# Attention and routed experts on one core: maxima placed in halves of a batch, second scores six steps behind the first

## The chip, the cores and the metric

The kernel runs on one core of one Trainium2 chip. The metric is the device time of one execution in microseconds. Engines: PE multiplies matrices, DVE (vector), ACT (scalar) and POOL (GpSimd) work on tiles, SP starts transfers. Each engine runs its own list of instructions in order and meets the others only through semaphores.

## The reference, cut to what matters

```python
# x, ctx: (8, 256, 256); 16 heads of 16; 8 experts, top 2, hidden width 1024
x = x + attention(layernorm(x), ctx, ctx)          # scores, softmax over keys, values, Wo, bo
h = layernorm(x)
gate = softmax(h @ w_gate.T)                       # choose 2 of 8 experts for each of 2048 tokens
y = sum over chosen e of gate_e * (gelu(h @ W1[e] + b1[e]) @ W2[e] + b2[e])
out = x + y
```

## The kernel before, in words

**Attention** goes over 8 batches of 256 tokens. The 16 heads of a batch are taken in 8 pairs, and a pair is one *step*, so that steps 0 to 63 hold the first scores of all pairs. In step s PE computes the scores of pair s into `S1` (`scores_for_max`, L1318), and DVE takes each query's maximum (`take_max`, L863) and stores it in `nmax`. PE cannot start the next `S1` before DVE has read this one. When a batch's 8 pairs are through, `maxima` (L872, L874) splits the 8 columns of maxima in two parts into `mrep`, PE turns them (`turn_maxima`, L1294), ACT copies them to `mT`, and a DMA from ACT's queue puts them into spare rows of the stacked queries `Q` (`maxima_out`, L1124). With these rows in place, a second product gives scores that already have the maximum taken off.

That product (`scores`, L1341, into `S2`) runs `LAG = 10` steps behind: step s holds the second scores of pair s - 10. ACT takes the exponential into `prob` (L1143), PE multiplies by the values two steps later, for two pairs at once (`weighted`, L1353), and ACT takes the sums out (`sums_out`, tile `OT`).

**Everything else is placed by tables of step numbers.** `FRONT` places a batch's loads, norm and projections (`xn` L1270, `q` and `k` L1278, `v` L1286) relative to step 8n. `BACK` and `LATE_BACK` place what follows the sums: division (`div` L1361, `divide`), turn and output projection (`ao`, `o`), residual (`add`), second norm (`ln2`, `norm2`), turn (`y`). `ROUTE` and `LATE_ROUTE` place the routing of groups of batches, (0, 1), (2, 3), (4), (5), (6), (7): `logits` L1370, `choose`, `gates`, `tags`, `count` L1385, `places` L947, `rows` L965, and `scatter` (L575), in which POOL issues one indirect DMA for each of 2 halves and 2 choices of a batch, so 4 for a batch, 8 for a group of two. Each engine's program walks the same steps and writes, in a fixed order within the step, what the table names. Nothing but semaphores ties engines to a step: an engine whose next work is ready goes on.

Batch 7 has its first scores in steps 56 to 63 and its second in 66 to 73. In steps 0 to 9, where there are no second scores, PE also runs matmuls that nobody reads (`unread`, L1391): 12 in step 0, 3 in each of the others.

**Experts** start at `UNIT_STEP = 76`: 23 tiles of up to 256 rows, each in 4 units (`pe_unit`, L1218 and L1233), one unit a step until step 99 and the rest after it. The expert and first row of a tile come from a table that DVE works out when the groups before it are routed (`LISTED`: the first 5 tiles after group 3 at step 70, two more after group 4, the others after group 5). SP loads rows and weights of a tile at the steps of `SP_TILES` (tiles 0 and 1 at step 71).

## Time and profile before

| | us |
|---|---|
| median of 3 runs (lowest, highest) | 524.69 (522.09, 527.28) |
| profiled execution | 525.33 |
| its span, first to last instruction | 524.0 |
| PE / DVE / ACT / POOL busy in the span | 457.9 / 360.4 / 334.8 / 165.2 |
| first `S1` matmul, last `S1` matmul | 23.7, 185.4 |
| last exponential, first expert matmul | 233.3, 241.7 |

The span is what the profiler saw of one execution. A busy share of PE is not PE at its peak, since matmuls overlap in its pipeline and their ends are modelled.

### The profile page before, as it was taken

How to read it: one execution, taken by the hardware profiler on the slowest of the kernel's cores; microseconds unless marked ns; L12 is line 12 of the kernel's file. 1: busy time of each engine (PE TensorE's matmuls, PEld its weight loads, DVE VectorE, ACT ScalarE, POOL GpSimd, SP SyncE). 2: the span in 40 equal slices, each digit the busy share in tenths (PEclk: the TensorE clock that was granted, in tenths of full speed). 3: DMA queues.
4: the chain of work that ended last, by engine and by line, in shares of the span. 5: the costliest groups of instructions: out<-in, count | busy, mean ns of one | idle time of the engine just before them, and what ended most of it. 6: DMA issues, size and time to landing. Idle time of an engine off the chain costs nothing.

```text
span 524.0 us, 10489 instructions
## 1 busy us (share of the span) xinstructions
PE 457.9 (87%) x3741; PEld 390.5 (75%) x3741; DVE 360.4 (69%) x791; ACT 334.8 (64%) x569; POOL 165.2 (32%) x213
## 2 busy tenths in 40 slices
PE   4897989999999844658889987999999999999993
PEld 3365666766765622427889977899999999999992
DVE  3276776776777751336977997298868788888862
ACT  1123776667666522335968856498779889889880
POOL 6023330352321577210361513132333213312323
PEclk9999999999999966665989989899999999999998
DMA  6557615324310023149275859859787987878822
GB/s 226 175 159 218 210 62 171 124 69 150 124 66 24 31 95 106 42 164 357 83 246 176 278 154 269 254 206 270 218 242 240 277 250 232 276 266 245 282 32 30
DMA packets 44356, 93.03 MB, mean 178 GB/s; under 512 B 6928, under 2 KB 30096, under 8 KB 38416
## 3 DMA queue, kind: packets, MB, share of 16 engines
q1 hardware_dynamic: 35072, 81.41, 46.3%
q0 software_dynamic: 7152, 9.46, 9.3%
q10 hardware_dynamic: 2080, 1.49, 0.9%
q8 instruction: 31, 0.51, 0.4%
q14 instruction: 21, 0.17, 0.1%
HBM read 63.01 MB, written 14.26 MB: 147 GB/s over the span
## 4 chain that ended last, share of the span: by engine, by line
PE 52%; issue 10%; DVE 10%; ACT 9%; DMA 6%; POOL 4%; another core or an unknown queue 4%; SPq 3%; ACTq 1%; DVEq 0%; POOLq 0%
PE S L1218 13%; PE bank L1233 12%; PE bank L1278 6%; PE bank L1286 5%; PE S L1318 4%; DMA w_in<-in_W 4%; PE bank L1353 3%; DVE nmax L863 3%; ACT hf L1068 2%; PE S L1391 2%; PE bank L1270 2%; PE S L1341 2%; ACT W2p L1049 2%; ACT Q L1037 1%
## 5 line engine op out<-in xcount | busy, mean ns | idle before, releaser
L1218 PE MATMUL S<-xgT,Q 128*128 128x256 f32 (+1 forms) x736 | 139.1, 289 | 8.7 <-DVE xgT L757 5.2
L534 POOL DMA_INDIRECT out<-y,slot x39 | 69.4, 1780 | 177.3 <-DVE y L781 103.7
L1218 PEld LDWEIGHTS S<-xgT,Q 128*128 128x128 f32 x736 | 117.5, 198 | 9.3 <-issue 9.3
L863 DVE TENSOR_REDUCE nmax<-S 128x4 f32<-128x1024 f32 x64 | 78.4, 1225 | 47.6 <-PE S L1318 45.1
L1218 PE MATMUL S<-xgT,K 128*128 128x256 f32 (+1 forms) x368 | 105.6, 287 | 0.0
L1068 ACT ACTIVATE hf<-S,b1c 128x256 f32<-128x256 f32 (+1 forms) x184 | 70.6, 435 | 40.2 <-PE S L1218 36.4
L1143 ACT ACTIVATE prob<-S 128x1024 f32<-128x1024 f32 x64 | 65.8, 1028 | 38.8 <-PE S L1341 27.7
L767 DVE TENSOR_TENSOR hp<-hf,hp 128x512 fp32r<-128x512 f32 (+1 forms) x92 | 55.8, 607 | 29.7 <-ACT hp L1081 29.3
L1218 PEld LDWEIGHTS S<-xgT,K 128*128 128x128 f32 x368 | 72.6, 197 | 0.0
L734 DVE TENSOR_TENSOR K<-w_in,Q 128x1024 fp32r<-128x1024 f32 x46 | 56.4, 1225 | 19.9 <-ACT Q L1037 19.9
L1233 PE MATMUL bank<-W2p,hp 128*128 128x256 f32 x528 | 67.6, 284 | 0.3 <-DVE y L777 0.3
L1233 PEld LDWEIGHTS bank<-W2p,hp 128*128 128x128 f32 x528 | 64.7, 191 | 0.6 <-issue 0.4
L554 POOL TENSOR_TENSOR rstd<-ve,half 128x2 f32<-128x2 f32 x16 | 11.8, 736 | 137.7 <-DVE ve L848 137.3
L1081 ACT ACTIVATE hp<-hf 128x512 fp32r<-128x512 f32 (+1 forms) x92 | 52.3, 569 | 2.9
L1037 ACT ACTIVATE Q<-w_in 128x1024 fp32r<-128x1024 f32 x46 | 48.2, 1048 | 8.6 <-DMA w_in<-in_W 7.5
L1233 PE MATMUL bank<-Q,hp 128*128 128x256 f32 x272 | 51.3, 282 | 1.3 <-DVE y L777 1.2
L1233 PEld LDWEIGHTS bank<-Q,hp 128*128 128x128 f32 x272 | 42.9, 188 | 1.6 <-issue 1.6
L575 POOL DMA_INDIRECT lists<-x2n,rows x32 | 31.7, 990 | 39.3 <-DVE rows L965 31.1
L1353 PE MATMUL bank<-prob,V 128*32 128x256 f32 x512 | 37.7, 416 | 1.2 <-ACT prob L1143 1.2
L1233 PE MATMUL bank<-K,hp 128*128 128x256 f32 x136 | 38.3, 282 | 0.0
L1318 PEld LDWEIGHTS S<-K,Q 64*128 64x128 f32 x256 | 19.1, 184 | 24.8 <-issue 13.2
L1318 PE MATMUL S<-K,Q 64*128 64x256 f32 x256 | 32.2, 330 | 5.7 <-DVE nmax L863 5.1
(179 smaller groups left out, 702.1 us busy)
## 6 DMA issues: line engine op xcount, KB each, us to landing
w_in<-in_W SPq DMA_DIRECT2D x46, 1024.0 KB, 7.9
K<-flat_k SPq DMA_DIRECT2D x24, 256.0 KB, 2.4
Q<-flat_q SPq DMA_DIRECT2D x24, 256.0 KB
xg<-lists SPq DMA_DIRECT2D x16, 265.0 KB
b_in<-in_b SPq DMA_DIRECT2D x23, 128.0 KB
lists<-zero SPq DMA_DIRECT2D x9, 265.0 KB, 4.9
cin<-in_ctxT SPq DMA_DIRECT2D x8, 256.0 KB, 3.5
xin<-in_x SPq DMA_DIRECT2D x8, 256.0 KB, 3.9
```

What stands on the lines that cost most here:

```text
L534: st_y[i % 4].after(pool.indirect_dma_start(out=out, out_offset=bass.IndirectOffsetOnAxis(ap=slot[i % 4][:, t:t + 1], axis=0), in_=y[i % 2 ...
L734: w1_lo.after(dve.tensor_tensor(W1p[i % 2][1][:, c], w1_in[i % 2][:, c], W1p[i % 2][0][:, c].bitcast(F32), ALU.subtract))
L767: h_lo.after(dve.tensor_tensor(hp[i % 2][1][:, c, 0:n], hf[pair % 2][:, :, 0:n], hp[i % 2][0][:, c, 0:n].bitcast(F32), ALU.subtract))
L863: max_done.after(dve.tensor_reduce(nmax[n % 4][:, :, :, m].rearrange("p t r -> p r t"), S1[:].rearrange("p r (t k) -> p r t k", t=TT), AX. ...
L1037: w1_hi.after(act.activation(W1p[i % 2][0][:, c], w1_in[i % 2][:, c], ACT.Copy))
L1068: h_act.after(act.activation(hf[pair % 2][:, u, 0:n], h_bank[pair][:, u, 0:n], ACT.Gelu, bias=b1c[i % 3][:, 2 * pair + u:2 * pair + u + 1]))
L1081: h_hi.after(act.activation(hp[i % 2][0][:, 2 * pair:2 * pair + 2, 0:n], hf[pair % 2][:, :, 0:n], ACT.Copy))
L1143: exp_done.after(act.activation(prob[s % 4][:].rearrange("p r t l -> p (r t l)"), S2[:].rearrange("p r l -> p (r l)"), ACT.Exp, scale=SCALE))
L1218: ins = pe.matmul(h_bank[pair][:, u, 0:n], W1p[k][a][:, kc, m * P:(m + 1) * P], xgT[k][c][:, kc, 0:n], start=(j == 0), stop=(j == len(term ...
L1233: ins = pe.matmul(y_bank[:, t, :], hp[k][a][:, m, t * P:(t + 1) * P], W2p[k][c][:, m, :], start=(j == 0), stop=(j == len(terms) - 1))
L1318: i = pe.matmul(S1[:, r, t * L:(t + 1) * L], Q[n % HELD][a, m, t * P:(t + 1) * P], K[n % HELD][a, m, :], start=not masked, stop=(not maske ...
L1353: i = pe.matmul(b[j * OS:(j + 1) * OS, 0:L], V[n % 3][:, t, r * MP + m, :], prob[(MP * n + m) % 4][:, r, t, :], start=(t == 0), stop=(t == ...
```

## The change: what it does

Maxima are handled in halves of a batch, 4 pairs each: `mrep0` and `mx0` after pair 3, `mrep1` and `mx1` after pair 7, each with its own turn, copy and DMA into half of the spare rows. The second scores wait for their half alone, and `LAG` is 6. The back work of a batch moves three to eight steps forward, the routing of groups 1 to 5 three to six, `UNIT_STEP`, `LAST`, `SP_TILES` and `POOL_TILES` four. Group 0 is routed 16 steps earlier, and its 8 scatters are written one to a step. Those of groups 1, 2 and 4 are written two to a step. Batches 5 and 7 are normalised on DVE, as batch 6 was. `xn` and `xT` come one step earlier, and ACT takes the values out ahead of the exponential.

```diff
-    UNIT_STEP = 76
+    UNIT_STEP = 72
-    LAG = 10
+    LAG = 6
+    MH = MP // 2
-    FRONT = dict(... xn=-8, xT=-7, ... v=-1, v_out=0, mrep=7, mx=8)
+    FRONT = dict(... xn=-9, xT=-8, ... v=-1, v_out=0)
-    BACK = dict(div=20, divide=21, ao=22, aT=23, o=27, add=28, store=30, ln2=32, norm2=33, y=34, yT=35)
+    BACK = dict(div=16, divide=17, ao=18, aT=19, o=19, add=20, store=22, ln2=24, norm2=25, y=28, yT=29)
-        6: dict(div=67, divide=67, ao=68, aT=69, o=69, add=70, store=71, ln2=71, norm2=71, y=72, yT=73),
+        6: dict(div=63, divide=63, ao=64, aT=65, o=65, add=66, store=67, ln2=67, norm2=67, norm_dve=67, y=69, yT=70),
-        1: dict(logits=60, choose=60, gate_exp=61, gates=62, tags=62, count=62, places=62, rows=63, scatter=63),
-        2: dict(logits=63, choose=63, gate_exp=64, gates=65, tags=65, count=65, places=65, rows=65, scatter=66),
+        0: dict(logits=38, choose=39, gate_exp=40, gates=42, tags=43, count=44, places=45, rows=46),
+        1: dict(logits=54, choose=55, gate_exp=56, gates=57, tags=57, count=57, places=58, rows=58),
+        2: dict(logits=59, choose=59, gate_exp=60, gates=61, tags=61, count=61, places=61, rows=61),
+    SCATTERS = {0: (46, 1), 1: (59, 2), 2: (63, 2), 3: (66, 4), 4: (74, 2), 5: (86, 4)}
+        for h in range(2):
+            due[MP * n + MH * (h + 1) - 1][f"mrep{h}"] = n
+            due[MP * n + MH * (h + 1)][f"mx{h}"] = n
...
             def scores(s):
-                if m == 0:
-                    pe.wait_ge(*stacked(m_stacked, n, 1))
+                if m % MH == 0:
+                    pe.wait_ge(m_stacked[n % HELD].sem, 16 * (2 * (n // HELD) + m // MH + 1))
...
+                for i, (first_step, each) in SCATTERS.items():
+                    for k in range(each):
+                        scatter(i, (s - first_step) * each + k)
...
+                if "v_out" in now:
+                    values_out(now["v_out"])
                 if 0 <= s - LAG < NP:
                     exponentials(s - LAG)
...
-                if "v_out" in now:
-                    values_out(now["v_out"])
```

**POOL, from the first scatter on, before.** L554 and L565 are a batch's inverse deviation and norm (`x2n`), L575 a scatter; x7 stands for seven in a row.

```order
L575 DMA lists<-x2n,rows 18688x265 [waits x2n_tag,rows_done]
L575 DMA lists<-x2n,rows 18688x265 x7
L554 TENSOR_TENSOR rstd<-ve,half 128x2 [waits ln_out1,ln_ve1]
L565 TENSOR_SCALAR x2n<-x,mv,rstd 128x256 [waits st_list0,pe_misc,ln_rstd1]
L565 TENSOR_SCALAR x2n<-x,mv,rstd 128x256
L575 DMA lists<-x2n,rows 18688x265 [waits x2n_tag,rows_done]
L575 DMA lists<-x2n,rows 18688x265 x7
L575 DMA lists<-x2n,rows 18688x265 [waits x2n_tag,rows_done]
L575 DMA lists<-x2n,rows 18688x265 x3
L575 DMA lists<-x2n,rows 18688x265 [waits x2n_tag,rows_done]
L575 DMA lists<-x2n,rows 18688x265 x3
```

**POOL at the same place, after** (L559, L567 and L579 are the same operations):

```order
L579 DMA lists<-x2n,rows 18688x265 x2
L559 TENSOR_TENSOR rstd<-ve,half 128x2 [waits ln_out1,ln_ve1]
L567 TENSOR_SCALAR x2n<-x,mv,rstd 128x256 [waits ln_rstd1]
L567 TENSOR_SCALAR x2n<-x,mv,rstd 128x256
L579 DMA lists<-x2n,rows 18688x265 x5
L559 TENSOR_TENSOR rstd<-ve,half 128x2 [waits ln_out1,ln_ve1]
L567 TENSOR_SCALAR x2n<-x,mv,rstd 128x256 [waits ln_rstd1]
L567 TENSOR_SCALAR x2n<-x,mv,rstd 128x256
L559 TENSOR_TENSOR rstd<-ve,half 128x2 [waits ln_out1,ln_ve1]
L579 DMA lists<-x2n,rows 18688x265 [waits x2n_tag,rows_done]
L579 DMA lists<-x2n,rows 18688x265 x7
L579 DMA lists<-x2n,rows 18688x265 [waits x2n_tag,rows_done]
```

The run of 8 of group 0 is now 3 (the first of them stands just ahead of these rows), a batch's norm, and 5. Group 1's 8 and group 2's 4, of which the last row is the first, still stand with nothing between them, although the table writes two to a step.

**PE from step 6 of a batch (its number modulo 8) to step 0 of the next, before** (L1318 first scores, L1341 second scores, L1353 values, L1270 a turn, L1286 the value projection, L1294 the maxima's turn):

```order
L1353 MATMUL bank<-prob,V 32x256 x8
L1270 MATMUL bank<-ident,ao 128x128 x4
L1318 MATMUL S<-K,Q 128x256 x4
L1341 MATMUL S<-Q,K 128x256 x4
L1286 MATMUL bank<-WvT,cin 128x256 x4
L1294 MATMUL bank<-ident,mrep 32x128 x2
L1318 MATMUL S<-K,Q 128x256 x4
L1341 MATMUL S<-Q,K 128x256 x4
L1353 MATMUL bank<-prob,V 32x256 x8
L1270 MATMUL bank<-ident,xn 128x128 x4
L1318 MATMUL S<-K,Q 128x256 x4
L1341 MATMUL S<-Q,K 128x256 x4
```

**PE at the same place, after** (L1329, L1352, L1364, L1281, L1297 and L1305, and L1372, the division's turn):

```order
L1364 MATMUL bank<-prob,V 32x256 x8
L1329 MATMUL S<-K,Q 128x256 x4
L1352 MATMUL S<-Q,K 128x256 x4
L1281 MATMUL bank<-ident,xn 128x128 x4
L1297 MATMUL bank<-WvT,cin 128x256 x4
L1305 MATMUL bank<-ident,mrep 16x128 x2
L1329 MATMUL S<-K,Q 128x256 x4
L1352 MATMUL S<-Q,K 128x256 x4
L1372 MATMUL bank<-ident,OT 128x128 x8
L1364 MATMUL bank<-prob,V 32x256 x8
L1329 MATMUL S<-K,Q 128x256 x4
L1352 MATMUL S<-Q,K 128x256 x4
```

Step 6 has lost the turn L1270 and holds only both scores and one product with values; step 7 has the turn of `xn` beside the value projection; the division's turn (L1372) stands in step 0, ahead of the product L1364.

**ACT at a batch's first step, before:**

```order
L1143 ACTIVATE prob<-S 128x1024
L1102 ACTIVATE mT<-bank 32x256
L1124 DMA Q<-mT 4x8x256
L1143 ACTIVATE prob<-S 128x1024
L1102 ACTIVATE OT<-bank 128x256
L1102 ACTIVATE V<-bank 128x32x16
L1102 ACTIVATE xT<-bank 128x512
L1143 ACTIVATE prob<-S 128x1024
```

**ACT at the same place, after:**

```order
L1153 ACTIVATE prob<-S 128x1024
L1109 ACTIVATE mT<-bank 16x256
L1133 DMA Q<-mT 4x4x256
L1109 ACTIVATE xT<-bank 128x512
L1109 ACTIVATE V<-bank 128x32x16
L1153 ACTIVATE prob<-S 128x1024
L1109 ACTIVATE OT<-bank 128x256
```

`xT` and `V` now stand between the DMA's issue and the exponential, which was ahead of both.

## Rows read from the trace of the kernel before

**Rows 1.** Stretches: length, busy us of PE, PEld, DVE, ACT, POOL, clock, DMA.
```profile
48.80:186.90 138.10, 130.17 (x1228) 91.43 (x1226) 99.31 (x195) 90.19 (x133) 43.48 (x46) 1.00 0.31 105
186.90:193.80 6.90, 0.04 (x1) 0.04 (x2) 3.91 (x18) 1.02 (x1) 5.62 (x7) 0.62 0.31 110
193.80:215.40 21.60, 10.48 (x76) 6.51 (x76) 4.65 (x30) 5.94 (x10) 12.50 (x13) 0.58 0.23 78
215.40:241.74 26.34, 17.82 (x129) 10.46 (x128) 12.68 (x59) 12.29 (x17) 4.56 (x5) 0.63 0.45 164
```

**Rows 2.** Timeline of PE, batch 4's start: start, duration, line, operation [idle before <-releaser].
```profile
96.96 0.51 PE L1318 MATMUL S<-K,Q 64*128 64x256 f32 x4
...
97.63 1.07 PE L1353 MATMUL bank<-prob,V 128*32 128x256 f32 x16
...
101.72 0.38 PE L1294 MATMUL bank<-ident,mrep 128*32 128x128 f32 x2
...
102.03 0.50 PE L1318 MATMUL S<-K,Q 64*128 64x256 f32 x4
...
105.67 1.99 PE L1278 MATMUL bank<-xT,WqT 128*128 128x256 f32 x8 [0.65 <-ACT xT L1102]
```

**Rows 3.** Timeline of PE, from step 63 to step 68.
```profile
185.81 1.06 PE L1370 MATMUL bank<-WgT,yT 128*128 128x8 f32 x8
...
193.76 0.61 PE L1294 MATMUL bank<-ident,mrep 128*32 128x128 f32 x2 [6.89 <-DVE mrep L874]
...
199.94 0.51 PE L1341 MATMUL S<-Q,K 64*128 64x256 f32 x4 [0.99 <-issue]
...
204.23 0.80 PE L1341 MATMUL S<-Q,K 64*128 64x256 f32 x4 [1.66 <-ACT prob L1143]
...
213.50 1.97 PE L1361 MATMUL bank<-ident,OT 128*128 128x128 f32 x8 [8.48 <-ACT OT L1102]
...
215.40 0.79 PE L1341 MATMUL S<-Q,K 64*128 64x256 f32 x4
```

**Rows 4.** Timeline of ACT, the same steps and step 70.
```profile
192.52 1.02 ACT L1143 ACTIVATE prob<-S 128x1024 f32<-128x1024 f32 x1 [6.83 <-remote]
...
213.06 0.39 ACT L1102 ACTIVATE OT<-bank 128x256 f32<-128x256 f32 x1 [8.89 <-remote]
...
225.25 1.03 ACT L1143 ACTIVATE prob<-S 128x1024 f32<-128x1024 f32 x1 [1.09 <-PE S L1341]
```

**Rows 5.** Timeline of POOL: run of 8 (first, last), first of 12, first of 4.
```profile
181.00 1.23 POOL L575 DMA_INDIRECT lists<-x2n,rows  x1 [0.34 <-DVE rows L965]
...
190.14 0.96 POOL L575 DMA_INDIRECT lists<-x2n,rows  x1 [0.30 <-issue]
...
195.77 1.08 POOL L575 DMA_INDIRECT lists<-x2n,rows  x1 [1.13 <-DVE rows L965]
...
219.50 0.96 POOL L575 DMA_INDIRECT lists<-x2n,rows  x1 [8.72 <-DVE rows L965]
```

**Rows 6.** Timeline of DVE, a maximum of step 6.
```profile
38.73 1.23 DVE L863 TENSOR_REDUCE nmax<-S 128x4 f32<-128x1024 f32 x1 [0.60 <-PE S L1318]
```

**Rows 7.** Timeline of PE, filler passes ahead of step 0.
```profile
21.00 2.76 PE L1391 MATMUL S<-onesb 128*128 128x512 bf16 x12 [1.64 <-issue]
```

**Rows 8.** Timeline of ACT: values out, maxima out and their DMA.
```profile
104.52 0.61 ACT L1102 ACTIVATE V<-bank 128x512 f32<-128x512 f32 x1
...
194.46 0.37 ACT L1102 ACTIVATE mT<-bank 32x256 f32<-32x256 f32 x1 [0.92 <-PE bank L1294]
...
194.87 0.64 ACTq L1124 DMA_DIRECT2D Q<-mT  x1
```

**Rows 9.** Timeline, all engines, normalising batch 6 (DVE) and batch 7 (POOL).
```profile
230.66 0.74 DVE L854 TENSOR_SCALAR x2n<-x,mv,rstd 128x256 f32<-128x256 f32 x2 [0.94 <-POOL rstd L554]
...
264.25 4.75 POOL L565 TENSOR_SCALAR x2n<-x,mv,rstd 128x256 f32<-128x256 f32 x2
...
269.05 0.66 PE L1270 MATMUL bank<-ident,x2n 128*128 128x128 f32 x4 [1.90 <-POOL x2n L565]
```

More of the change, by code:

```diff
@@ new lines, in build @@
+    ROUTE = {
+        0: dict(logits=38, choose=39, gate_exp=40, gates=42, tags=43, count=44, places=45, rows=46),
+        1: dict(logits=54, choose=55, gate_exp=56, gates=57, tags=57, count=57, places=58, rows=58),
+        2: dict(logits=59, choose=59, gate_exp=60, gates=61, tags=61, count=61, places=61, rows=61),
+        3: dict(logits=62, choose=62, gate_exp=63, gates=64, tags=64, count=64, places=65, rows=65),
+        4: dict(logits=71, choose=71, gate_exp=72, gates=72, tags=72, count=73, places=73, rows=74),
+        5: dict(logits=82, choose=82, gate_exp=84, gates=84, tags=84, count=85, places=85, rows=85)}
@@ L134, in build @@
             due[FIRST_FRONT[n][name] if n in FIRST_FRONT else MP * n + o][name] = n
-        for name, o in BACK.items():
-            due[LATE_BACK[n][name] if n in LATE_BACK else MP * n + o][name] = n
+        for h in range(2):
+            due[MP * n + MH * (h + 1) - 1][f"mrep{h}"] = n
+            due[MP * n + MH * (h + 1)][f"mx{h}"] = n
+        for name, step in LATE_BACK[n].items() if n in LATE_BACK else [(k, MP * n + o) for k, o in BACK.items()]:
+            due[step][name] = n
     for i, ns in enumerate(GROUPS):
-        for name, o in ROUTE.items():
-            due[LATE_ROUTE[i][name] if i in LATE_ROUTE else MP * ns[-1] + o][name] = i
+        for name, step in ROUTE[i].items():
+            due[step][name] = i
     for stage, (i, step) in LISTED.items():
@@ L519, in pool_constants @@
             return pool_const.value
[L521 removed]
+        POOL_TILES = {80: 0, 84: 1, 88: 2, 92: 3}
         def add_to_output(i):
@@ L566, in normalise, with scatter @@
                                                            ALU.subtract, ALU.mult))
-            def scatter(i):
+            def scatter(i, d):
                 ns = GROUPS[i]
-                pool.wait_ge(rows_done.sem, 2 * (i + 1))
-                pool.wait_ge(x2n_tag.sem, 2 * (i + 1))
-                for u, n in enumerate(ns):
-                    for t in range(TT):
-                        for k in range(TOP):
-                            st_list[n % KEPT].after(pool.indirect_dma_start(
-                                out=lists, out_offset=bass.IndirectOffsetOnAxis(
-                                    ap=rows[i % 2][:, k, u * TT + t:u * TT + t + 1], axis=0),
-                                in_=x2n[:, n % KEPT, t], in_offset=None))
+                if not 0 <= d < len(ns) * TT * TOP:
+                    return
+                u, t, k = d // (TT * TOP), d // TOP % TT, d % TOP
+                if d == 0:
+                    pool.wait_ge(rows_done.sem, 2 * (i + 1))
+                    pool.wait_ge(x2n_tag.sem, 2 * (i + 1))
+                n = ns[u]
+                st_list[n % KEPT].after(pool.indirect_dma_start(
+                    out=lists, out_offset=bass.IndirectOffsetOnAxis(
+                        ap=rows[i % 2][:, k, u * TT + t:u * TT + t + 1], axis=0),
+                    in_=x2n[:, n % KEPT, t], in_offset=None))
             pool_r.after(pool.memset(taken[:], 0.0))
@@ L851, in normalise @@
                 dve.wait_ge(ln_rstd[which].sem, n + 1)
+                if which and n >= KEPT:
+                    dve.wait_ge(pe_misc.sem, filled_by("y", n - KEPT))
+                    dve.wait_ge(st_list[n % KEPT].sem, 16 * TT * TOP * (n // KEPT))
                 for t in range(TT):
@@ L972, in dve_attention @@
                     take_max(s)
-                if "mrep" in now:
-                    maxima(now["mrep"])
+                for h in range(2):
+                    if f"mrep{h}" in now:
+                        maxima(now[f"mrep{h}"], h)
                 if s == FLAG:
@@ L1158, in act_attention @@
                 act_loads(s)
-                if "mx" in now:
-                    maxima_out(now["mx"])
+                for h in range(2):
+                    if f"mx{h}" in now:
+                        maxima_out(now[f"mx{h}"], h)
                 if "aT" in now:
@@ L1402, in pe_attention @@
                     unread(UNREAD.get(s, 3 if s > 0 else 0))
-                if "mx" in now:
-                    turn_maxima(now["mx"])
+                for h in range(2):
+                    if f"mx{h}" in now:
+                        turn_maxima(now[f"mx{h}"], h)
                 if 0 <= s < NP:
```

90 lines of the change are left out of this document (40 added, 50 removed).

## Prediction, made blind

> **What bounds the kernel now.** I read the stretches first [rows 1], then the timeline of PE through them [rows 2, 3], then who waited [rows 4], then POOL [rows 5]. From the first second scores to step 63, PE is busy 130.2 of 138.1 us at full clock: this stretch is bound by PE's own work, 138.1 over 54 steps, 2.56 each, about 20.5 for a batch of 8. Then come 54.8 us, to the first expert matmul at 241.7, in which PE works 28.3 us, mostly at half clock (granted 0.58 to 0.63) [rows 1]. They hold steps 64 to 75: ten second scores without first ones, plus the back work of batches 5 and 6 and the routing that gives the first expert table. Behind 241.7 the experts keep PE nearly full, so a microsecond off this point is a microsecond off the end, if the expert stretch itself does not grow.
>
> The 54.8 us have two big holes. PE finishes group 2's logits at 186.9 and does nothing for 6.89 us. It starts the second scores of step 67 at 204.2 and the next work at 213.5, after 8.48 us of idleness; before them 0.99 and 1.66 us [rows 3]. In both holes the others wait for PE and PE for them: ACT's exponential starts at 192.5 after 6.83 us, although PE's logits, which stand behind its scores, are recorded at 185.8, and `OT` starts at 213.06 after 8.89 us, although PE's record is past its product by 204.2 [rows 3, 4]. What goes beside the holes is POOL: eight scatters in a row from 181.0 to 191.1, twelve from 195.8 to 210.8 (219.50 less 8.72) [rows 5]. Each hole opens about four microseconds after its run of scatters starts and closes one to two after it ends. I take it that a long run of indirect DMAs holds back what PE signals; the trace shows only that they coincide. The run of four from 219.5 has a small one, 1.09 us [rows 4, 5].
>
> **Part 1, four steps fewer.** Steps 64 to 67 took 193.76 to 215.40, 21.6 us [rows 3]. In the changed order what stands in them is done by step 63, where first scores run too. There it costs PE's slots at full clock: both scores of a step start 0.67 us before the next thing, so one is 0.33; a product with values 1.0; the maxima's turn 0.31 [rows 2]; logits of a single batch 1.0; the division's turn, 1.9 from start to next start at half clock, 0.95 [rows 3]; a turn of `x2n` some 0.6 [rows 9]. Sum: 4 x 0.33 + 2 x 1.0 + 0.31 + 0.6 + 1.0 + 0.95 + 0.3 for the short matmuls of two counts (an estimate) = 6.5. **-21.6 + 6.5 = -15.1.** Step s of the tail then does what s + 4 did, and tail queues move with it: SP's tile loads, stores and the table stand in the same order to each other. SP's later waits, and POOL's output adds, keep their distance to the units. I leave the half clock of 215 to 242 as it is [rows 1].
>
> **Part 2, filler and halves.** Twelve filler passes go (four steps with three), 2.76 us [rows 7]; their place is taken by second scores that bring work, so I count -2.8. Eight more turns of maxima cost PE 0.31 each [rows 2]: +2.5. DVE's two short operations, ACT's copy of 0.37 and the 0.64 us of its DMA issue [rows 8] double as well, but in the steady stretch DVE is busy 72% and ACT 65% [rows 1], so PE's own queue hides them. What if that cover is gone: ACT then pays about 1.0 us eight times. Sum **-0.3.**
>
> The added wait is that of the fifth pair's second scores for the second half. Behind it on PE stand the next products and the next first scores, and so DVE. Between the issue of the copy and the need lie two steps before and after, some 5 us. The worst case in the trace is the last copy, issued at 194.87 among scatters, whose scores started at 199.94 with 0.99 us of waiting [rows 3, 8]; elsewhere PE shows no wait there. Bounds: 0 and 16 x 0.99 = 16. I take 0, as the seven other copies are nearest.
>
> On copying in halves a page has a rule: the Trainium skill, "DMA: Bandwidth & Descriptors", Rules for kernel authors, says to coalesce small transfers, since below 64 KB one pays mostly overhead. The copy was 32 KB and becomes twice 16. By that rule each half takes nearly as long as the whole, which costs nothing while two steps cover it, and by the rule the sum would stay as it is up to the third rival below.
>
> **Part 3, the uneven steps.** In step 6 of a batch only both scores and one product are left, 1.67 us of PE. A first-score step cannot go round faster than DVE's maximum and the scores ahead of it, 1.23 + 0.60 = 1.83 us [rows 6]: +0.16 in each of 7 batches, +1.1. In step 0 the product with values takes the bank of the value projection, which ACT must empty behind `mT`, the DMA issue and `xT`: the turn's 0.38 [rows 2], 0.37, 0.64, and 0.6 each for `xT` and `V` [rows 8] put this at about 2.65 us after the step begins, while PE is there at 0.31 + 0.67 + 0.95 = 1.93. That is +0.7 seven times, +4.9. Against it, PE waits for `xT` ahead of the query projection now, 0.65 us in five batches [rows 2], and `xT` comes before the exponential then: -3.3. Bounds: 0 to 6.0; sum **+2.7.**
>
> **Part 4, the scatters.** The table writes them one or two to a step, but POOL has nothing in between that waits, so the lists decide. They show 3, then a batch's norm, then 5; then 8 and 4 adjacent; then 4. I price a run by the nearest row: 8 costs 6.9, 4 costs 1.1, 5 between them 2.5, and 3 nothing. Whether 8 and 4 join to 12 depends on group 2's rows, which need the count of step 61: PE would be held there, as in the first hole [rows 4], so they should come apart. After: 2.5 + 6.9 + 1.1 = 10.5 and the unchanged run of group 3. Part 1 took away 11.1 (0.99 + 1.66 + 8.48 [rows 3]) with steps 64 to 67, and 6.9 lay ahead of them: so 10.5 - 6.9 = **+3.6.** Bounds: -6.9 (no stall left) and +11.1 (the holes stay whole: 18.0 in place of 6.9).
>
> A page speaks against the cause that I name: the Trainium skill, "SBUF — State Buffer", section "SBUF: two separate sides", says that the ports of engines and of DMAs are disjoint and that PE never waits for another's. By this rule the holes would come from something else that keeps its place in the steps, and the sum would take the upper bound. The trace shows both holes beside the long runs and no others of their size, so I go by the runs.
>
> **Part 5, the norms.** Batch 7's norm took POOL 4.75 us and PE waited 1.90 for it; on DVE batch 6's took 0.74 [rows 9]. DVE waits about 0.9 for `rstd` in exchange. The wait goes, and next is the output projection, already there: **-1.9.** Batch 5's lies in the PE-bound stretch: 0. Moving back work and group 0's routing forward within that stretch changes no sum.
>
> **Sum:** -15.1 - 0.3 + 2.7 + 3.6 - 1.9 = **-11.0 us** on the profiled execution's 525.3, so 514.3. It stands 0.6 above the median of 524.69; I give **513.7**.
>
> **Rivals.** *The scatters no longer hold PE back* (3, 5, 8 and 4 are short enough, or PE's tighter loop rides over them): part 4 gives -6.9 in place of +3.6, 503. For it: the fours cost next to nothing. Against: a run of eight did cost 6.9. Chance 0.2.
> *The stalls stay whole,* since 8 and 4 join while first scores still run, or since something else makes them: 18 us in place of 10.5, and the uneven steps at their upper bound, +3.3: 11 us more, 524. Chance 0.18.
> *Slower: the halves land late.* PE meets a copy's semaphore 16 times and not 8, ahead of first scores. It decides when copy and turn take over 5 us; at 0.99 x 16 = 16 us more than forecast, the time is 529.7, and with the uneven steps at their bound 533. Against: one wait in eight. Chance 0.06.
> *The change doesn't do what it says:* the steps before 64 fill so much that the tail's work is merely moved, at the same half clock elsewhere; as PE is dense there at full clock, I give this 0.04, at 522.
> My forecast's own case has 0.52, from 508 to 519 by its bounds.
>
> **The numbers.** 502 to 523 holds the forecast, the first rival and most of the second. A measurement of this kernel tells about 1% from no change: faster means below 519.4. Forecast, first rival and a fifth of the others: 0.78 faster; within 1% 0.16; slower 0.06.
>
> **What would show it.** The last first scores near 190 (185.4 before, plus 6.5 - 0.3 + 2.7, less what gaps take up), then a hole of 6 to 8 us beside eight scatters around steps 60 to 63 and none of 8.5 at step 67; 1.1 us or less at the four. The first expert matmul near 232. PE's wait for `xT` gone and one of about 0.7 before the product of step 0 in its place. No wait on the maxima's semaphore. No PE wait for `x2n` of batch 7. I am wrong if the holes do not follow the runs of scatters, or if the steady stretch costs more than 21.5 us for a batch.

## The result: slower by 1.2%, and the profile after

The changed kernel takes 532.92 us (median of 4 runs, 529.61 to 534.13), the kernel before 525.65 beside it: a ratio of 1.0122, 95% interval 1.0067 to 1.0177. The forecast was 513.7 and its range ended at 523.0. The profiled execution took 532.52, 7.2 more than the 525.3 of before, where the sum had said 11.0 less: 18.2 us to be found. Medians here are of all executions; ratios and their intervals leave out those more than 1.5% above the fastest of their kernel.

The stretches of the kernel after, with the columns of [rows 1]: from the first second scores to the last first scores (step 63), from there to the first expert matmul, and the rest; then from DVE's maximum of step 0 to the first expert matmul.

```profile
43.16:214.44 171.28, 153.36 (x1329) 105.54 (x1329) 113.78 (x259) 99.92 (x151) 60.59 (x63) 0.93 0.30 101
214.44:245.84 31.40, 18.83 (x141) 12.29 (x141) 15.59 (x70) 13.68 (x20) 7.50 (x9) 0.66 0.53 199
245.84:531.00 285.16, 263.36 (x2158) 261.14 (x2158) 217.73 (x452) 216.19 (x394) 78.72 (x48) 0.96 0.72 213
...
22.35:245.84 223.49, 184.94 (x1539) 125.81 (x1537) 141.79 (x345) 117.34 (x178) 71.64 (x76) 0.89 0.37 123
```

The tail did get shorter, as planned: 31.4 us, where before 56.6 lay between the first scores of step 63 and the experts. The loss is ahead of it: the last first scores start at 214.4, where the forecast had them near 190. The rows of before, the tail and from step 0 to the experts, in which PE is busy 179.58 of 217.51 us:

```profile
185.14:241.74 56.60, 30.06 (x222) 18.52 (x219) 21.50 (x107) 19.64 (x29) 24.13 (x25) 0.62 0.35 125
24.23:241.74 217.51, 179.58 (x1540) 121.29 (x1538) 137.80 (x327) 114.39 (x170) 73.75 (x78) 0.90 0.36 119
```

After, PE idles about as much (38.6 against 37.9) and is busy 5.4 longer with the same number of matmuls. So the stalls were moved, not removed, and some of the work runs at the lower clock. The largest of them, on PE's timeline after (start, duration, line, operation, in brackets the idle time ahead and what ended it), with the DMA ahead of it on SP and the next maximum on DVE:

```profile
38.46 0.65 SPq L453 DMA_DIRECT2D K<-line  x1
...
43.16 0.80 PE L1352 MATMUL S<-Q,K 64*128 64x256 f32 x4 [6.14 <-DMA K<-line]
43.88 3.78 PE L1297 MATMUL bank<-WvT,cin 128*128 128x256 f32 x8
...
48.43 1.23 DVE L871 TENSOR_REDUCE nmax<-S 128x4 f32<-128x1024 f32 x1 [10.15 <-PE S L1329]
```

These are the first second scores, now at step 6. `scores(0)` waits for all four `k_ones`, and the last copy of `line` into K is issued at step 5 of SP's list and lands 4.6 us later. In the kernel before, at step 10, PE shows no wait there. The kernel before already held the price: there the last copy is issued at 40.40 (SP's timeline), between the first scores of step 6 (38.18) and of step 7 (41.19), so that second scores moved to step 6 had to meet it. The value projection behind the wait takes 3.78 us in place of the 1.99 of such a one at full clock, and DVE stands idle for 10.15 us. Later on PE, in order:

```profile
73.31 0.63 PE L1372 MATMUL bank<-ident,OT 128*128 128x128 f32 x4 [0.69 <-ACT xT L1109]
...
172.05 0.60 PE L1305 MATMUL bank<-ident,mrep 128*16 128x128 f32 x2 [2.76 <-issue]
...
187.56 0.38 PE L1305 MATMUL bank<-ident,mrep 128*16 128x128 f32 x2 [1.83 <-DVE lg L931]
...
201.27 0.39 PE L1305 MATMUL bank<-ident,mrep 128*16 128x128 f32 x2 [2.68 <-DVE mrep L883]
...
208.41 0.50 PE L1329 MATMUL S<-K,Q 64*128 64x256 f32 x4 [2.12 <-DVE nmax L871]
...
215.60 1.97 PE L1372 MATMUL bank<-ident,OT 128*128 128x128 f32 x8
...
228.41 0.50 PE L1352 MATMUL S<-Q,K 64*128 64x256 f32 x4 [2.75 <-ACT prob L1153]
...
245.84 0.76 PE L1229 MATMUL S<-xgT,Q 128*128 128x256 f32 x2 [3.32 <-DVE xgT L762]
...
253.45 0.17 PE L1396 MATMUL bank<-chosen,before 128*128 128x8 bf16 x1 [3.01 <-DVE ao L901]
```

Against [rows 3]: the holes of 6.89 and 8.48 are gone; in their place stand three waits for the maxima's turn (L1305, at steps 52, 56 and 60, 7.3 us), 2.12 ahead of the first scores of step 62, 3.32 at the first unit with 4.90 ahead of it (shown below), and one at a count (L1396). The scatters that answer to [rows 5] start at 158.31 (three, then five), 199.94 (eight), 213.53 and 221.65 (four each).

### The profile page after: what moved, and what is told of

The parts are those of the page before. It is cut to its first block, busy times and chain, and to the rows that moved or that the text cites. A ratio compares the mean times of both kernels' runs of the same rounds, so it can differ in the third digit from the quotient of the medians.

```text
span 531.2 us, 10563 instructions
## 1 busy us (share of the span) xinstructions
PE 461.9 (87%) x3745; PEld 395.2 (74%) x3745; DVE 365.5 (69%) x811; ACT 337.6 (64%) x577; POOL 158.3 (30%) x209
## 4 chain that ended last, share of the span: by engine, by line
PE 62%; DVE 11%; ACT 7%; issue 7%; DMA 6%; SPq 3%; POOL 2%; ACTq 1%; another core or an unknown queue 1%; DVEq 0%; POOLq 0%
PE S L1229 17%; PE bank L1244 14%; PE bank L1289 6%; PE bank L1297 5%; PE S L1329 5%; PE bank L1364 4%; DVE nmax L871 3%; DMA w_in<-in_W 3%; PE bank L1281 2%; PE S L1352 2%; ACT hf L1075 2%; ACT Q L1044 1%; PE bank L1211 1%; PE S L1402 1%; PE bank L1381 1%
## 5 line engine op out<-in xcount | busy, mean ns | idle before, releaser
L1044 ACT ACTIVATE Q<-w_in 128x1024 fp32r<-128x1024 f32 x46 | 48.2, 1047 | 16.6 <-DMA w_in<-in_W 16.6
L559 POOL TENSOR_TENSOR rstd<-ve,half 128x2 f32<-128x2 f32 x16 | 11.8, 737 | 138.0 <-DVE ve L853 136.8
L579 POOL DMA_INDIRECT lists<-x2n,rows x32 | 31.9, 998 | 49.9 <-DVE rows L974 41.9
L1329 PE MATMUL S<-K,Q 64*128 64x256 f32 x256 | 33.7, 343 | 6.0 <-DVE nmax L871 5.3
L1329 PEld LDWEIGHTS S<-K,Q 64*128 64x128 f32 x256 | 20.1, 194 | 25.0 <-issue 13.9
L1364 PE MATMUL bank<-prob,V 128*32 128x256 f32 x512 | 38.3, 422 | 0.0
```

The costliest lines, as they stand in the source:

```text
L1044: w1_hi.after(act.activation(W1p[i % 2][0][:, c], w1_in[i % 2][:, c], ACT.Copy))
L1329: i = pe.matmul(S1[:, r, t * L:(t + 1) * L], Q[n % HELD][a, m, t * P:(t + 1) * P], K[n % HELD][a, m, :], start=not masked, stop=(not maske ...
L1364: i = pe.matmul(b[j * OS:(j + 1) * OS, 0:L], V[n % 3][:, t, r * MP + m, :], prob[(MP * n + m) % 4][:, r, t, :], start=(t == 0), stop=(t == ...
```

## Experiments

The groups of runs lay on different chips, and each has its own runs of the kernel before: chip A 525.2 and 523.9 us, chips B, C and D 513.1, 512.2 and 512.6. Ratios are to those. The record names no chip for the two profiles and the result above; their times are like those of chip A. First kernels on chip A.

**The wait for the spare rows: `own_ones`.** The wait is there since `prob` lies over `line`; so `line` moves.

```diff
-                if s == 0:
-                    for ones in k_ones:
-                        pe.wait_ge(ones.sem, 16)
...
-            line = sb(first, "line", [2 * D, L])
+        line = sb(top, "line", [2 * D, L])
```

> The changed kernel, with memory of its own for `line` (the source of the spare rows of K), so that the first second scores need not wait until all four copies of it have landed. Theory: the wait of 6.14 us in the changed kernel at step 6 stands only because `prob` lies over `line`, and the 8.5 us by which step 8 comes later there are new cost of the change. The hole goes, what follows keeps its distances: 532.9 - 8 = about 525, the same as before. Rival: the time to the first expert matmul is set by the routing of the fourth group or by the tile loads, and an earlier start is given back later: 530 or more, with the first expert matmul still near 245.

518.89 us, ratio 0.9877 (0.9795 to 0.9958): the changed kernel without this wait is faster than the kernel before on chip A. The hole is gone, and the next four stalls (0.69, 2.76, 1.83, 2.68) stand as they were. The first expert matmul is at 235.9. The rival is out.

**Halves alone: `halves`.** The kernel before with this and the functions `turn_maxima`, `maxima`, `maxima_out` and the waits of the change, `LAG = 10` and the old tables.

```diff
-    FRONT = dict(... mrep=7, mx=8)
+        for h in range(2):
+            due[MP * n + MH * (h + 1) - 1][f"mrep{h}"] = n
+            due[MP * n + MH * (h + 1)][f"mx{h}"] = n
```

> The kernel before, with the maxima turned and copied in halves of a batch and nothing else: second scores still ten steps behind, all tables as they were. Theory of the prediction: 8 more turns on PE at 0.31 us, else nothing: about +2.5 us, no PE wait for the copies. Rival (halves land late): up to 16 us slower. Rival (cover by PE's queue is complete, since DVE's maximum sets the pace): 0.

532.0 us, ratio 1.0169 (1.0077 to 1.0262), 2.7 times what the theory gave. No wait for the copies. A batch in steps 24 to 32 takes 0.92 us longer. 0.31 of that is the turn; the rest is a wait ahead of the product with values at the second turn:

```profile
94.13 1.07 PE L1363 MATMUL bank<-prob,V 128*32 128x256 f32 x16 [0.66 <-DVE x L906]
```

The extra turn takes one more of the four banks in rotation, so the product gets the bank of the output projection, which DVE has not emptied yet. Four such waits make 2.6 us, eight turns 2.5, and a new wait for DVE ahead of the turn of step 20 makes 1.5. (In the changed kernel the tables give other banks, and there this row isn't.)

**Runs of scatters: `paced` and `run8`.** Both on top of `own_ones`, the first with the first two of these lines, the second with the third.

```diff
+                        if i == 0 and 0 <= s - first_step < 8:
+                            pool.wait_ge(max_done.sem, s)
...
-    SCATTERS = {0: (46, 1), ...
+    SCATTERS = {0: (49, 8), ...
```

> The changed kernel with memory of its own for `line`, and the eight scatters of the first group at steps 48 to 55, each behind a wait for that step's predecessor's maximum, so that they are truly one to a step (some 2.6 us apart) instead of runs of 3 and 5. Theory (a run of indirect DMAs holds back what PE signals): the idle time of PE beside them (2.76 us in the changed kernel, 5 in a row) goes, 2 to 3 us less than with memory of its own alone. Rival (the number counts, not the run): the same sum of idle time, spread. Rival (the wait ahead of the maxima's turn comes from DVE's routing work): the 2.8 us stay.

> The changed kernel with memory of its own for `line`, and the eight scatters of the first group in one row at step 49. Theory (runs hold PE back, eight in a row cost 6.9 us in the kernel before): PE idle beside them some 7 us in place of 2.8, the time 4 us over that with memory of its own alone. Rival (runs are not the cause): within 1 us of it.

`paced` 521.85, ratio 0.9917 (0.9874 to 0.9959): no gain, and its gap at step 52 is still 2.77. But POOL was held up by a norm, and three scatters stood in a row there after all, so it tells little. `run8` 525.33, ratio 0.9960 (0.9909 to 1.0010): the eight make a hole that three and five did not, 3.86 us and not 7, while the gap at step 52 shrinks to 1.51:

```profile
164.98 0.96 POOL L579 DMA_INDIRECT lists<-x2n,rows  x1 [0.31 <-issue]
...
168.52 1.03 ACT L1153 ACTIVATE prob<-S 128x1024 f32<-128x1024 f32 x1
...
169.16 0.79 PE L1329 MATMUL S<-K,Q 64*128 64x256 f32 x4 [3.86 <-DVE nmax L871]
```

PE's semaphore updates for work that ended at 162.1 to 165.3 all stand in the trace at 167.7 to 168.0, 2.8 us and more behind the start of the last scatter: up to 5.6 us late. (ACT's next work on what PE made, `OT`, starts at 167.76 after 5.05 us of idleness; what ended up to 161.1 was still taken up at once.) The time is 6.4 us over that of `own_ones` by the medians, but the two intervals overlap.

**Chip B: `probe`, `xt_first`, `count72`, `three_fixes`.** The probe, in POOL's loop (the eight indirect DMAs at 34 to 41 likewise):

```diff
+                if s in (18, 26):
+                    pool.wait_ge(max_done.sem, s)
+                    for k in range(8):
+                        if s == 18:
+                            st_probe.after(pool.dma_start(probe_rows[k * P:(k + 1) * P], zero[:, 0]))
+                        else:
+                            probe(8 + k)
```

> The changed kernel with memory of its own for `line`, and 24 writes of 128 rows of `zero` to a scratch tensor in DRAM that nobody reads, of the scatters' size, from POOL, in the steady stretch where POOL and PE had nothing of the kind: eight ordinary DMAs in a row at step 18, eight indirect ones in a row at step 26, eight indirect ones at steps 34 to 41, each behind the wait for its step's maximum. One profile shows all three places. Theory (a run of indirect DMAs holds back PE's signals): no hole at step 18, PE's records of semaphores late by several us and a hole of 3 to 7 us at steps 26 to 30, nothing at 34 to 41. Rival 1 (any DMA of POOL's queue does it): holes at 18 and at 26. Rival 2 (routing work, not scatters, made the holes): none of over 1 us at any of the three, each of the batches 2 to 4 costs the 21.1 to 23 us that it did. Rival 3 (each indirect DMA costs, in a row or not): holes at 26 and at 34 to 41 alike.

516.8 (one run, before 513.07). Here neither place has a hole, and with eight indirect DMAs from 91.78 to 101.8 no update of PE is late. (The record of the one for second scores that end at 94.51 is missing from the trace, but ACT's exponential, which waits for it, starts at 94.55.) What does cost is the queue: `xn` of the next batch stands behind them on POOL, and PE waits 1.03 us for it. On this chip eight and twelve scatters in a row hold nothing back in `three_fixes` either, so the probe can't tell indirect from ordinary DMAs where the effect exists.

`xt_first`, in ACT's step, and `count72`; `three_fixes` has both:

```diff
+                if "xT" in now:
+                    evacuate("xn", now["xT"], xT[:], halves)
                 for h in range(2):
                     if f"mx{h}" in now:
                         maxima_out(now[f"mx{h}"], h)
...
-        4: dict(... tags=72, count=73, places=73, rows=74),
+        4: dict(... tags=72, count=72, places=72, rows=74),
```

> The changed kernel with memory of its own for `line`, and ACT empties `xT` ahead of the copy and the DMA of the maxima in the steps where both stand. Theory: in each batch PE waits 0.67 us ahead of the second turn of the division because its bank is that of `xn`, which ACT empties only behind the maxima's copy (0.37) and DMA issue (0.64). The five gaps of 0.67 go: 3 us less (about 516). Rival: the next wait (for `V`, one place on) takes their place: no change.

> The changed kernel with memory of its own for `line`, and the count of the fifth group at step 72 in place of 73, ahead of the last batch's division as it was in the kernel before (76 against 77). Theory: PE's wait of 3.0 to 3.7 us ahead of that count, beside the first tile's units, comes only of the two banks that the division takes first and DVE gives back behind its work for the experts. It goes, 3 us less (about 516). Rival: the wait for DVE's `hp` of the first unit takes its place, no change.

> The changed kernel with memory of its own for `line`, `xT` ahead of the maxima's copy on ACT and the count at step 72, all three. Theory: the gains add, 518.9 - 3 - 3 = about 513, the number that the prediction gave for a change without these three conflicts. Rival: they lie one behind the other, 516 or more.

`xt_first` 510.75, ratio 0.9978 (0.9938 to 1.0017); `count72` 508.14, 0.9903 (0.9869 to 0.9936); both together 505.87, 0.9855 (0.9810 to 0.9899). By the medians `xT` first is worth 2.3 us on top of the count, and the count 4.9 on top of `xT`. The kernel with neither was not run on this chip. Beside its ratio on chip D, 1.0010, the two are worth 1.6 and 5.5 us and both together 7.9, so they add as far as ratios from two chips can tell. In `xt_first` PE now waits 0.17 at that place, for `V`, which was the rival, at a quarter of the size.

With the count ahead of the division its wait is 1.45 for `chosen` and that of the first unit 1.56 in place of 3.3: the wait of 3.0 to 3.7 was for banks only.

**Chip A again: `before_traced`, `own_ones_again`, `w1_late`, `five_fixes`.** `w1_late` is `three_fixes` and

```diff
-                if s in (UNIT_STEP - 3, UNIT_STEP - 2):
-                    w1_high(0, s - UNIT_STEP + 3)
                 if s == UNIT_STEP - 1:
+                    w1_high(0, 0)
+                    w1_high(0, 1)
```

with the same for `w1_low`; `five_fixes` has `rows=59` for the second group besides.

> The kernel before, profiled beside the kernels of this group, since its time differs between groups (525 and 513 us). Theory (the holes beside the scatters belong to the chip or its moment): in a group in which it takes 513, its two holes of 6.89 and 8.48 us are small or gone and the rest of its timeline is the same to 1 us; in a group in which it takes 525, they are there. Rival (the whole program runs evenly slower, by the clock or the DMAs): both holes stand, the other stretches differ.

> The changed kernel with memory of its own for `line`, once more, to have it beside the ones that build on it. Its ratio to the kernel before was 0.988 when that took 525; if part of its gain were of that group alone (its holes beside scatters are shorter than those of the kernel before), the ratio is nearer to 0.99 to 0.995 where the kernel before takes 513.

> The changed kernel with memory of its own for `line`, `xT` first, the count at step 72, and the first tile's two conversions of W1 on ACT and DVE at step 71 in place of 69 and 70. Theory: ACT stands 4.9 us in its queue before the conversion for weights that are still on their way, with `yT` of batch 6 and an `OT` behind it, and PE with 3.2 to 4.9 us ahead of the first tile's turn waits for that `yT`. Without it PE does the turn and the logits of the fifth group at once, and only the weights' landing and the conversions hold the first unit: 1 to 3 us less than with the three edits. Rival: the first unit needs the conversions anyway, and these now come later: no change or 1 us more.

> As the one before, and the second group's rows on DVE at step 59 in place of 58, behind the maximum and the halves' copy. Theory: the gap of 2.68 us ahead of the maxima's turn of step 60 stands because DVE's routing of step 58 lies ahead of the maximum of step 59; it shrinks by 0.8 us (four short operations), some 1 us less than the one before. Rival: nothing, since DVE's norm and statistics fill the same place.

`before_traced` (529.89, one run) shows the two holes again, 6.94 and 8.55. `own_ones_again` 519.68, 0.9919 (0.9878 to 0.9960). `w1_late` 509.63, **0.9719** (0.9675 to 0.9762). In the changed kernel the first tile looks like this:

```profile
238.25 1.06 ACT L1044 ACTIVATE Q<-w_in 128x1024 fp32r<-128x1024 f32 x1 [6.36 <-DMA w_in<-in_W]
239.21 0.58 ACT L1109 ACTIVATE yT<-bank 128x512 f32<-128x512 f32 x1
...
239.93 1.08 PE L1211 MATMUL bank<-ident,xg 128*128 128x128 f32 x4 [4.90 <-ACT yT L1109]
```

ACT stands 6.36 us ahead of the conversion of weights still on their way, `yT` behind it, and PE behind `yT`. The cause lies in the table: `yT` of batch 6 moved three steps forward, from 73 to 70, and the conversion four, from 73 to 69, so that it now stands ahead of `yT` on ACT; in the kernel before `yT` (232.67) came ahead of it (235.96). In `w1_late` PE's wait at the turn is gone, and the first unit's is 2.87, where `three_fixes` has 1.56. As `three_fixes` was not run on chip A, what this edit is worth by itself is not measured.

`five_fixes` is 517.32, 0.9878 (0.9839 to 0.9917): one table entry, meant to save 0.8 us, costs 7.7. The gap at the turn did shrink, from 2.67 to 1.98. But the later rows let the second and third group's scatters join to twelve:

```profile
190.60 1.09 POOL L579 DMA_INDIRECT lists<-x2n,rows  x1 [3.48 <-DVE rows L974]
...
204.66 0.96 POOL L579 DMA_INDIRECT lists<-x2n,rows  x1 [0.30 <-issue]
205.00 0.38 ACT L1109 ACTIVATE OT<-bank 128x256 f32<-128x256 f32 x1 [9.00 <-remote]
205.44 1.97 PE L1369 MATMUL bank<-ident,OT 128*128 128x128 f32 x8 [7.94 <-ACT OT L1109]
207.99 1.02 ACT L1153 ACTIVATE prob<-S 128x1024 f32<-128x1024 f32 x1 [2.60 <-remote]
...
210.83 0.60 PE L1305 MATMUL bank<-ident,mrep 128*16 128x128 f32 x2 [3.42 <-DVE mrep L883]
```

This is the hole of 8.48 of [rows 3] again, in another kernel in which the runs joined to twelve; updates for logits and scores of PE that ended at 196.6 to 197.5 stand at 207.9 and 208.0, 11.3 us late at most.

**Chip C: `w1_again`, `pause4`, `turn_later`, `both`.** `pause4` adds a wait of POOL ahead of two scatters, `turn_later` puts `turn_maxima` behind `scores` in PE's step, `both` has both.

```diff
+    PAUSES = {(0, 5): 53, (1, 4): 61}
...
+                if (i, d) in PAUSES:
+                    pool.wait_ge(max_done.sem, PAUSES[i, d])
```

> The kernel with four edits (memory for `line`, `xT` first, count at step 72, first conversions at step 71) once more, as the one that the three others of this group change. 0.972 to 0.985 of the kernel before.

> The four edits, and POOL waits for the maximum of step 52 ahead of the sixth scatter of the first group and for that of step 60 ahead of the fifth of the second: runs of 3, 2, 3 and 4, 4, 4 in place of 3, 5 and 8, 4. Theory (the length of a run decides): the gap of 3.5 us after the count of the second group and half of the 2.7 us at step 52 go, 3 to 4 us less than the four edits alone where those holes are there. Rival (the sum of scatters decides, or something else than scatters): no change, or the signals come back only behind the last of them.

> The four edits, and PE turns a half of the maxima behind both scores of its step, not ahead of them. Theory: at steps 4 and 8 of a batch the turn waits for the maximum of the step before and for the two short operations behind it, 0.4 us, and keeps both scores waiting with it. With the scores ahead, each gap of 1.5 to 2.7 us (four of them) loses about 0.4 us and the turn fills another: 1 to 3 us less. Rival: the copy lands 0.9 us later, so that the second scores two steps on wait for it: no change or slower.

> The four edits with the pauses and the later turn. If the gains add, 4 to 6 us less than the four edits alone.

`w1_again` 500.41, 0.9761 (0.9720 to 0.9801). `pause4` 502.9, 0.9811 (0.9757 to 0.9865): no gain, but on this chip there are no holes to take away, and the second group's pause was already met. `turn_later` 508.24, 0.9901 (0.9858 to 0.9945), slower by 1.4%: most of the gaps at steps 4 and 8 only move behind the turn, and the product with values now waits in every batch, 0.99 to 1.02 us, for ACT to empty `V`. `both` 506.72, 0.9881 (0.9842 to 0.9920). The same program `w1_late` needs 208.8 us from step 0 to the first unit on chip A and 196.8 on chip C. PE at the place of the hole that chip A has (3.51), among twelve scatters on chip C:

```profile
190.03 0.96 POOL L579 DMA_INDIRECT lists<-x2n,rows  x1 [0.30 <-issue]
...
191.98 0.50 PE L1329 MATMUL S<-K,Q 64*128 64x256 f32 x4 [0.84 <-DVE nmax L871]
```

**Chip D: `after_again`, `own_ones_third`.**

> The changed kernel once more, beside the one with memory of its own for `line`. Its ratio to the kernel before was 1.012 where that took 525. If the holes beside scatters are what differs between groups, and the kernel before loses more in them (15.4 us in two holes, the changed one some 8), it is 1.02 to 1.03 in a group where the kernel before takes 512, and 1.01 again in one where it takes 525.

> The changed kernel with memory of its own for `line`, in the same group. Theory: 8.5 to 10.5 us less than the changed kernel (the wait and the half clock behind it), 0.98 of it. Rival: the 12.8 us that the two earlier ratios give are right.

524.69, ratio 1.0217 (1.0131 to 1.0303), and 513.21, ratio 1.0010 (0.9980 to 1.0040). The first came as expected. Side by side the wait costs 11.5 us by the medians (0.978), some 10.6 by the ratios: a little more than the theory and less than the 12.8 of the rival. The change is worse by a per cent more on a chip where the changed kernel has no holes beside scatters. Stretches of each (`after_again` first): steps 0 to 8, 32 to 40, 40 to 56, 56 to 63, from 63 to the first unit.

```profile
24.05:53.44 29.39, 19.41 (x102) 12.58 (x100) 14.98 (x26) 6.76 (x11) 3.54 (x5) 0.83 0.53 147
116.43:141.01 24.58, 23.88 (x204) 17.20 (x200) 17.22 (x38) 14.53 (x22) 7.66 (x8) 0.93 0.30 103
141.01:189.69 48.68, 45.11 (x398) 31.49 (x394) 34.98 (x86) 28.94 (x44) 20.37 (x21) 0.93 0.29 98
189.69:211.40 21.71, 17.76 (x185) 11.81 (x182) 16.47 (x57) 11.49 (x20) 11.25 (x12) 0.92 0.19 65
211.40:238.64 27.24, 15.29 (x130) 9.48 (x129) 14.47 (x64) 13.13 (x20) 7.49 (x9) 0.76 0.56 208
```

```profile
20.91:41.55 20.64, 17.20 (x111) 11.21 (x113) 15.08 (x26) 6.82 (x12) 3.55 (x5) 1.00 0.68 186
103.92:126.89 22.97, 22.27 (x204) 15.99 (x200) 17.16 (x39) 14.53 (x22) 7.66 (x8) 1.00 0.33 110
126.89:173.78 46.89, 41.79 (x398) 29.38 (x394) 34.91 (x87) 28.66 (x44) 20.37 (x21) 1.00 0.30 101
173.78:195.50 21.72, 17.78 (x185) 11.94 (x182) 16.46 (x56) 11.49 (x20) 11.25 (x12) 0.92 0.19 65
195.50:223.99 28.49, 15.29 (x131) 9.48 (x129) 14.48 (x64) 13.13 (x20) 7.50 (x9) 0.82 0.61 218
```

The hole costs 8.75 by step 8. 1.6 and 1.8 more come at steps 32 to 56, which hold the same work with PE's clock granted at 0.93 on the mean in place of 1.00. The hole is not needed for that: the same 0.93 over steps 32 to 40 stands in the profile of `w1_late` on chip A and not in that of the same program on chip C, both without the hole. It is a short stretch at the lower of the two levels (0.50), in which one value projection takes 3.48 us in place of 1.89. PE shows no idle time in it or in the eight microseconds ahead. `w1_late`, then `w1_again`:

```profile
114.00:118.00 4.00, 4.00 (x36) 2.80 (x30) 2.46 (x3) 3.83 (x7) 3.90 (x5) 1.00 0.01 4
118.00:122.00 4.00, 4.00 (x49) 3.13 (x48) 2.02 (x3) 1.89 (x3) 0.01 (x1) 1.00 0.55 197
122.00:126.00 4.00, 4.00 (x14) 3.11 (x14) 3.00 (x10) 1.51 (x2) 0.00 (x0) 0.57 0.20 69
...
122.52 3.48 PE L1297 MATMUL bank<-WvT,cin 128*128 128x256 f32 x8
...
102.70:126.69 23.99, 23.77 (x204) 17.17 (x200) 17.23 (x38) 14.53 (x22) 7.67 (x8) 0.93 0.31 105
```

```profile
124.79 1.89 PE L1297 MATMUL bank<-WvT,cin 128*128 128x256 f32 x8
...
105.06:127.44 22.38, 22.16 (x204) 16.00 (x200) 17.16 (x39) 14.53 (x23) 7.66 (x8) 1.00 0.34 113
```

Both profiles of the changed kernel have such a stretch in steps 32 to 40, and of the versions without the wait for the spare rows `paced` and `w1_late` have it, while `own_ones` in three profiles, `run8` and `w1_again` do not.

The same program on a chip with late updates and on one without shows what they cost, as far as two single profiles can tell. `own_ones` on chip A, to be held against the last three rows of `own_ones_third` above:

```profile
130.03:179.73 49.70, 43.35 (x398) 29.98 (x394) 34.95 (x88) 28.90 (x44) 20.38 (x21) 0.97 0.28 96
179.73:207.10 27.37, 20.34 (x182) 13.44 (x179) 16.62 (x56) 11.13 (x19) 13.05 (x14) 0.77 0.18 62
207.10:235.93 28.83, 17.73 (x133) 10.87 (x132) 14.53 (x64) 13.57 (x20) 5.61 (x7) 0.68 0.51 184
```

The stretch with scatters in runs of three and five takes 2.8 us more, that with eight 5.7 more, the last 0.3 more. Of these 8.8 only 2.2 are idle time of PE. In the other 6.6 it is busy longer with the same matmuls, at a clock that is lower on the mean (0.97, 0.77 and 0.68 in place of 1.00, 0.92 and 0.82). On chip D eight and four join to twelve, from 184.2 to 199.4, and PE shows no hole beside them.

## Why the prediction was wrong, step by step

The step that failed: the sum put at nothing every wait that the moved work would meet. It has no term for what the first second scores wait for when they move from step 10 to step 6, it let "PE's own queue" hide the waits ahead of the maxima's turns, and it took the last steps to do after the change what they did before.

| | before, us | after, us | more | forecast |
|---|---|---|---|---|
| start to the first `S1` | 23.7 | 21.8 | -1.9 | 0 |
| to the division's turn (before 213.50, after 215.60) | 189.8 | 193.8 | +4.0 | -9.1 |
| to the first expert matmul | 28.2 | 30.2 | +2.0 | 0 |
| to the end | 282.3 | 285.4 | +3.1 | -1.9 |

The turn is that of step 67 before and of step 63 after; behind it the same work follows. The first row is in no part of the forecast; the profiles of all versions start step 0 between 20.0 and 23.7.

- **Not in any part: the first second scores meet the spare rows, 8.75 us by the traces, 11.5 by the medians.** It is the largest single piece. I had costed the move of second scores from step 10 to 6 by the filler that they replace (part 2, -2.8) and had not asked what `scores(0)` waits for: a line of the kernel, and a row of SP's timeline (40.40, above).
- **Part 1, four steps fewer, -15.1.** The tail lost 25.2 (56.6 to 31.4), so the main term held. What failed is its sentence that step s of the tail then does what s + 4 did. The count of the fifth group went from 76 to 73, behind the last division on two banks: 3.0 us in this profile, 4.9 by the medians of `three_fixes` against `xt_first`. And between SP's reading of the first table and the first unit stand 16.6 us, where before it was 13.2 (229.2 to 245.8, 228.5 to 241.7): the conversion that waits for the weights now stands ahead of `yT` on ACT, and PE waits 4.90 + 3.32 at the first tile, where in the kernel before it was 0.50 and 1.73.
- **Part 2, cover.** 0.31 for a turn was right. That "PE's own queue hides" DVE's two short operations was not: at steps 52, 56, 60 and 64 the turn's wait is 1.51, 1.83, 2.68 and 1.05 on chip D, 7.1 in all, where the kernel before has one such wait of 1.01 apart from the holes. That PE has too little else there and DVE too much routing is read from the timelines; no run took these waits away (`five_fixes` only shortened one, 2.67 to 1.98). The halves do land in time: the third rival gave 529.7 to 533 and the time is 532.9, but its reason, late copies, is not what happened, so that its nearness is luck. In the kernel before, halves cost 6.8 us by themselves, 2.5 of it the turns and 2.6 the rotation of banks, which I had not followed.
- **Part 3, uneven steps, +2.7.** Right in kind: the 0.65 for `xT` ahead of the query projection is gone and 0.67 to 0.69 stands in its place five times, for `xT` too and not for `V`, one instruction group earlier. Steps 24 to 32 take 21.18, before 20.37: 0.81 more, within the 21.5 that I had set as the bound. The bound does not hold further on: steps 32 to 40 take 24.6 (23.0 on chip D without the short stretch at the lower clock), 40 to 48 22.0 and 48 to 56 27.7.
- **Part 4, scatters, +3.6.** The order of the runs was right where the profile above was taken (3, 5, 8, 4, 4); on chip D it is 3, 5, 12, 4. By the waits alone the prices were too high: five in a row cost 1.3 (2.76 less the 1.51 that stand there without a held update), eight 2.1 (2.12 and 0.81, less the 0.88 of chip D), four 1.6 (2.75 less 1.12). With the lower clock beside them it is 8.8 in place of 10.5 on chip A, and nothing that the traces show on chips B to D, so the size was near by adding two things that I had not told apart. The reading that PE's holes open four microseconds behind the start of a run and close one to two behind its end was off: they open 5.9 and 9.2 behind it and close 2.7 behind the end. The mechanism was borne out on chip A by `run8` and `five_fixes`, and its second rival, that runs join, is what `five_fixes` is. The rule about ports of the Trainium skill, "SBUF — State Buffer", section "SBUF: two separate sides", weighed there, has not been contradicted: what is held back is PE's semaphore update, not its access.
- **Part 5, the norm, -1.9.** Right for the wait: none for `x2n` of batch 7. But the stretch in which it lay is 3.1 us longer, 3.0 of it the count.

The miss of 13.1 up to the division's turn: 8.8 for the spare rows and 1.7 for the short stretch at the lower clock in steps 32 to 40, which the profiles of the changed kernel and of `own_ones` differ by; 6.0 for the turns of steps 52, 56 and 60 as chip D has them; less 1.7 for the scatters. That is 14.8; the 1.7 too many I can't divide. Behind the turn, the first tile's waits are 6.0 longer ((4.90 + 3.32) less (1.73 + 0.50)), and others on the way 4.0 shorter. With the spare rows' wait and three other conflicts removed the changed order runs at 0.972 to 0.976, 12 to 14 us better than before. That this is near the forecast's 11.0 is in part luck: on chip C the sum's terms for the scatters don't exist, and the halves' waits are still in it.

## What to carry to other kernels

When work moves to an earlier step, list every semaphore that its code waits for, the one-time ones too, and look up in the trace when each is given: a wait that never showed can be the largest. Buffers laid over each other carry such waits from one end of the program to the other, and rotating banks carry them from any claim to the fourth after it. And when a tail is to shrink by moving a table of steps, check each entry against its old neighbours and the chain that the tail waits for: here one entry off by one cost 4.9 us, and another by one, in a repair, 7.7.

## What the runs showed of the chip

- On chip A semaphore updates of PE come late beside a long run of indirect DMAs on POOL, while PE goes on working: in `before_traced` by 6.7 us with eight in a row (second scores that ended at 185.3, recorded at 192.0) and by 11.7 with twelve (a product that ended at 200.85, whose `OT` starts at 212.57), until 2.4 to 3.3 us behind the start of the last one. That the run is the cause rests on `run8` and `five_fixes`, where a moved run moved the hole; why it does so is open. On chips B, C and D, among as many scatters, no update of PE is recorded over 0.9 us behind the end of the work before it. The kernel before takes 524 to 525 us on the one and 512 to 513 on the others; no profile of it was taken on B to D, so that its two holes make this difference is argued, not shown. Chips B to D had one group of runs each, so that chip and moment can't be told apart there.
- Hence the worth of a version depends on the chip: `own_ones` is at 0.988 and 0.992 on A and at 1.001 on D, the changed kernel at 1.012 on a chip that the record doesn't name and at 1.022 on D. A comparison of versions needs the same chip.
- PE's clock can fall to its lower level without idle time of PE: in `w1_late` the granted clock is 0.57 over 122 to 126, though PE is busy all the time from 114 on, and behind a row of logits (matmuls of 8 columns) the same work takes 1.6 us longer. In `w1_again`, the same program, it stays at 1.00. What decides it stays open; it is noise that a comparison of two single profiles has to leave out.
